# One signal a step from TensorE in an expert loop of 158 steps

## The reference

```python
diff = x[:, :, None, :] - keys
logits = -jnp.sum(diff * diff, axis=-1) + jnp.einsum('bld,ed->ble', x, rw) + rb
topv, topi = jax.lax.top_k(logits, TOP_K)
w = jax.nn.softmax(topv, axis=-1)
hidden = jax.nn.gelu(jnp.einsum('bld,efd->blef', x, w1) + b1, approximate=False)
exp_out = jnp.einsum('blef,edf->bled', hidden, w2) + b2
fused = jnp.sum(w[..., None] * jnp.take_along_axis(exp_out, topi[..., None], axis=2), axis=2)
```

## Time and profile before

| | us |
|---|---|
| three runs: lowest, median, highest | 754.55, 759.54, 760.06 |
| the profiled execution | 753.02 |
| its span, first to last instruction | 751.3 |

### The profile page before, as it was taken

The page is one execution under the profiler, slowest core; times in us unless marked ns, Lnnn a source line. Parts: engine busy times, 40 slices in busy tenths (PEclk is TensorE's granted clock), DMA queues, the critical chain, the costliest instruction groups (busy, mean ns, idle before and its releaser), DMA issues.

```text
span 751.3 us, 19912 instructions
## 1 busy us (share of the span) xinstructions
PE 543.2 (72%) x6240; PEld 492.2 (66%) x6242; DVE 364.9 (49%) x1325; ACT 356.8 (47%) x1079; POOL 281.9 (38%) x308
## 2 busy tenths in 40 slices
PE   4989889973127268777778996770895876799984
PEld 4958788952114158776667886770795865788952
DVE  5646599979993035524445651110133333343226
ACT  6433367756563035433445774330562443455623
POOL 3000000003616731454665445567225555545520
PEclk9999899996556679988999999686898789999997
DMA  8950000041013235333444654442365554456744
GB/s 230 252 230 3 2 2 0 0 177 48 1 70 115 82 88 147 92 116 110 131 115 141 211 152 134 114 126 71 102 201 173 181 178 122 139 150 189 218 164 137
DMA packets 55746, 92.28 MB, mean 123 GB/s; under 512 B 10352, under 2 KB 26096, under 8 KB 55152
## 3 DMA queue, kind: packets, MB, share of 16 engines
q1 hardware_dynamic: 45424, 72.35, 31.8%
q0 software_dynamic: 10240, 18.89, 8.4%
HBM read 78.07 MB, written 17.37 MB: 127 GB/s over the span
## 4 chain that ended last, share of the span: by engine, by line
PE 40%; DVE 16%; issue 14%; another core or an unknown queue 13%; ACT 7%; POOL 6%; DVEq 2%; DMA 2%; POOLq 0%; SPq 0%; ACTq 0%
PE bank L2144 14%; PE bank L2137 11%; POOL yd L596 5%; ACT value L879 3%; DVE shared L1183 2%; DVE shared L1175 2%; DVE early L1463 2%; DMA shared<-yd 1%; PE bank L1731 1%; PE bank L1836 1%; PE bank L1768 1%; PE bank L2129 1%; PE bank L1758 1%; PE bank L1999 1%
## 5 line engine op out<-in xcount | busy, mean ns | idle before, releaser
L879 ACT ACTIVATE value<-bank,shared 128x128 f32<-128x128 f32 x632 | 180.8, 373 | 252.3 <-remote 132.5
L2144 PE MATMUL bank<-shared,value 128*128 x1264 | 188.9, 297 | 98.5 <-ACT value L879 75.8
L2144 PEld LDWEIGHTS bank<-shared,value 128*128 128x128 f32 x1264 | 169.1, 208 | 109.5 <-issue 108.8
L596 POOL DMA_INDIRECT yd<-early x128 | 130.3, 1018 | 165.1 <-DVE early L1659 145.5
L2137 PE MATMUL bank<-early,shared 128*128 x1264 | 183.0, 290 | 7.7 <-issue 5.0
L2137 PEld LDWEIGHTS bank<-early,shared 128*128 128x128 f32 x1264 | 166.2, 205 | 8.5 <-issue 7.9
L1659 DVE SCALAR_TENSOR_TENSOR early<-bank,value,early 128x128 f32 x158 | 55.4, 351 | 231.2 <-PE bank L2144 110.1
L588 POOL DMA_INDIRECT shared<-xd,early x128 | 124.2, 970 | 86.4 <-issue 49.6
L559 POOL TENSOR_TENSOR shared<-shared,xn 128x512 f32<-128x512 f32 x4 | 5.1, 1267 | 174.4 <-DVE xn L1258 166.6
L2129 PE MATMUL bank<-ident,shared 128*128 128x128 f32 x128 | 36.3, 287 | 20.6 <-issue 15.7
L887 ACT ACTIVATE early<-bank 128x128 f32<-128x128 f32 x128 | 37.9, 299 | 7.7 <-remote 6.8
(11 more groups left out here) (334 smaller groups left out, 693.6 us busy)
## 6 DMA issues: line engine op xcount, KB each, us to landing
shared<-w1b SPq DMA_DIRECT2D x158, 258.0 KB
w1b<-in_w_t SPq DMA_DIRECT2D x1, 4096.0 KB, 17.4
shared<-col_dram SPq DMA_DIRECT2D x1, 4096.0 KB, 13.3
shared<-in_w_t SPq DMA_DIRECT2D x1, 4096.0 KB, 12.4
att<-yd SPq DMA_DIRECT2D x8, 512.0 KB
shared<-yd SPq DMA_DIRECT2D x4, 1024.0 KB, 9.5
xd<-xnT SPq DMA_DIRECT2D x2, 1280.0 KB
shared<-xd,early POOLq DMA_INDIRECT x128
```

What stands on the lines that cost most here:

```text
L596: pool.indirect_dma_start(out=yd[:, :], out_offset=bass.IndirectOffsetOnAxis(ap=idx_dst[:, m:m + 1], axis=0), in_=yg[:, m % SLOTS, :], in_ ...
L879: ins = act.activation(hT[:, i % 2, tok(c)], bank[2 + i % 2][:, tok(c)], ACT.Gelu, bias=w1_now[:, i % WR, F + c:F + c + 1])
L2144: ins = mm(bank[6 + i % 2][:, 0:D], hT[:, i % 2, tok(c)], w2_sb[:, bass.ds(e, 1), c, :] .rearrange("p a d -> p (a d)"), start=(c == 0), st ...
```

## The change

`xgT_ps` is signalled only by the transposes ahead of the loop (tiles 0 and 1), `down_ps` only by the last two second products. Every other reader of these two waits for `up_ps` instead, at the count of the first first-product that TensorE runs behind the transpose or second product in question: `turned(n)` and `summed(i)` give the semaphore and count. ACT's Gelu loses its wait for `down_ps`. In DVE's step `y_add` stands ahead of `bring`.

```diff
+        def turned(n):
+            if n < brought(0):
+                return xgT_ps, n + 1
+            i = next(i for i in range(IALL) if brought(i + 1) > n)
+            return up_ps, i + 2
+
+        def summed(i):
+            return (up_ps, i + 3) if i < IALL - 2 else (down_ps, i - IALL + 3)
...
             def gelu(i):
                 act.wait_ge(up_ps, i + 1)
-                freed(act, down_ps, i - 1)
...
             def xT_copy(n):
-                act.wait_ge(xgT_ps, n + 1)
+                act.wait_ge(*turned(n))
...
             def bring(g):
                 n, h = g * GRP, g * GRP // JT
-                dve.wait_ge(xgT_ps, n + GRP)
+                dve.wait_ge(*turned(n + GRP - 1))
...
             def y_add(i, e):
-                dve.wait_ge(down_ps, i + 1)
+                dve.wait_ge(*summed(i))
...
                 e = expert(dve, i - 2) if i >= 2 else None
+                if i >= 2:
+                    y_add(i - 2, e)
                 for g in range(brought(i) // GRP, brought(i + 1) // GRP):
                     bring(g)
-                if i >= 2:
-                    y_add(i - 2, e)
...
             def rows_T(n):
-                nc.tensor.transpose(bank[n % 2][:, 0:P], xg[:, n % XR, 0:D], ident[:, :]).then_inc(xgT_ps, 1)
+                ins = nc.tensor.transpose(bank[n % 2][:, 0:P], xg[:, n % XR, 0:D], ident[:, :])
+                if n < brought(0):
+                    ins.then_inc(xgT_ps, 1)
...
             def down(i, e):
-                ins.then_inc(down_ps, 1)
+                if i >= IALL - 2:
+                    ins.then_inc(down_ps, 1)
```

## The result

The changed kernel takes 776.3 us (median of 4 runs, 773.5 to 781.9) against 757.0 before: ratio 1.027, 95% interval 1.018 to 1.036. It is slower, where I had forecast 714 us. Times are medians of all runs, ratios go by the means of the fast runs alone, so the two can differ in the third digit.

The account below looks back on a forecast made before the run. The prediction took the kernel to be bound by TensorE signals arriving late while GpSimd issues indirect DMAs without pause. 753.0 - 52 (signals) + 12 (given back) = 713, stated as 714 us; range 668 to 762.

Parts of the forecast that it names:

- What bounds the kernel: Expert loop: TensorE's finished-product signals reach other engines late while GpSimd issues indirect DMAs without pause; one Gelu starts after 6.71 us idle.
- Signals, 29 + 12 + 8 + 3 = 52 us: Cutting TensorE's signals from 444 to 162 was to save 52 us, split over four kinds of loop stretch.
- two-call stretches: Loop at 307 to 395 and 560 to 650 us, two GpSimd calls a step: 3.40 to 2.85 us, saving 29.
- rival A: All TensorE signals: busy GpSimd shuts the path however many are sent; no gain, 753 to 768 us; chance 0.16 with D.
- D: TensorE's profile rows mislead: products ran late for weights, signals have no part; 753 to 768 us; chance 0.16 with rival A.
- Given back, 12 us: Later waits in ACT and DVE were to cost 12 us in total, range 0 to 50.
- the copy 11 where I had 6: ACT's copy before the Gelu: 0.29 us fits the cover; hot_lanes behind it cost 4 us, x2T copies 2.
- bring 25 where I had 6: DVE's bring waits for the next first product, delaying prepare and y_add: 0.6 us in some ten steps, 6 us.
- Rival B: Order of ACT and DVE waits costs more (49 us) than signals gain (17): 785 us, range 768 to 795; chance 0.12.
- What the profile would show: Signs if right: less unnamed Gelu idleness, two-call stretches from 0.29 to 0.35 steps per us, GpSimd's DVE wait lower, clock above 0.90.
- The stretch 395 to 460: Loop part between these times: longer than 2.3 us a step was a sign of Rival B.
- My first sign: ACT's Gelu: its idleness for unnamed releasers was to fall from 132.5 to under 90 us.

## Why the prediction was wrong

- **What bounds the kernel.** Right, as far as tested: the stands of the earlier trace rows come with GpSimd's indirect calls, since they go when the calls go (610 us) and the loads stay. What I could not see is that the same calls hold nothing at 613. That a hold ends when GpSimd pauses isn't so in every case (y_add at 512.35).
- **Signals, 29 + 12 + 8 + 3 = 52 us.** This is the step that failed. I priced every signal as a risk of its own. With all waits alike, 162 and 444 signals take 775.8 and 776.7 us, so 52 us measured about nothing. The two-call stretches took 87.7 and 89.5 us against my 72 and 77. A lone signal is held as three were; rival A had this right, at 0.16 with D, though not the time (753 to 768), since it took over my 12 us.
- **Given back, 12 us.** This term was mis-sized too. It measured 33 with no signal held (643.2 less 610.0), and 20 at 757, where the two-call stretches, which at 613 lose about 5 and 4 us, lose nothing. By parts, at 613: the copy 11 where I had 6, bring 25 where I had 6, y_add and the Gelu's wait about 2. For bring I counted only the steps with long prepares; its rows show a blocked DVE (2.27 us) in front of work that has its own deadline, and TensorE stands 29 us at the second products where it stood 15. For the copy I compared it with the Gelu's slack and left out the table products, which wait for the hot lanes behind it: the hot stretch grows by 6 us. And I had not seen that the transpose, which needs the copy, shortens how far TensorE can run past a held signal: 58.7 us of standing.
- **Rival B** had the sign and, by chance, the size (768 to 795): it let signals gain 17, which is 0, and charged 49 for the order, 37 of it for the copy, which is 20 in all.
- **What the profile would show.** The stretch 395 to 460 is above 2.3 us a step as B said (78.7 us for 28 steps, 2.8), and the second product's waits for the Gelu are many and short (21.3 us, 27 times), as B said too. My first sign came true all the same and meant nothing: ACT's unnamed idleness fell from 132.5 to 76 us in this profile (71.0 at the copy, 5.0 at the Gelu), but it is 107 in the second profile of the same kernel and 104 with all signals sent. GpSimd's wait for DVE rose, 145.5 to 161.1, where I had it fall; the two-call stretches kept 0.29 and 0.30 steps a microsecond, at a clock of 0.86 and 0.87.

## What to carry to other kernels

Before replacing an early signal by a later one, list for each waiting engine what is queued behind the wait and who needs that; the wait costs nothing only where the later signal has already come when the engine gets there, so move the waiting step as well (ACT's prepare ahead of its copies: 1.031 to 1.024; bring one step later: to 0.996). That a signal arrives late doesn't mean that there are too many: send them all with no one waiting, and the question is answered in one run, if the kernel before beside it shows the same late signals. Measure each kernel beside its own base: 757 and 613 us are the same kernel.

## What the runs showed of the hardware

The same kernel took 611 to 615 us in some rounds and 755 to 757 in others, and one chip number has both (14). At 757 ScalarE can start 20.3 us after the product that it waits for while GpSimd issues indirect DMAs back to back, and in the same stream VectorE 7.0 us after its own; with these calls replaced no wait has an unnamed releaser and the kernel takes 610 us, and at 613 there is none either, in spite of calls just as dense in the rows shown. A memset of 0.33 us behind each gather, with its own wait, takes the longest such wait from 24.4 to 5.5 us and the time from 748.8 to 723.3, in two rounds at 757; more memsets at 613 only cost. What differs between the rounds, and what holds the signal, no run here shows.

The Trainium skill ("VectorE: DVE Perf Modes", "The DRAIN you can't avoid") says that a semaphore costs nothing extra on VectorE; for TensorE these runs agree, 775.8 against 776.7 us.
